# x and out laid out in DRAM as in SBUF, the first tiles loaded whole and split by halves, unused matmuls ahead of and between the first tiles

## Chip, core and metric

The kernel runs on one core of one Trainium2 chip. The metric is device time in microseconds (us), the median of several executions. Besides these there is one profiled execution, from which every row below comes.

## What is computed

The reference takes x (8 batches of 1024 nodes with 128 features, f32) and adj (1024 x 1024). It has two layers, each `x = layernorm(x + layer(x))`.

- Layer 0: with A2 = adj*adj (element by element), `h = relu(A2 @ (x @ W1))`, `h = relu(A2 @ (h @ W2))`, `A2 @ (h @ W3)`. W1 is 128 x 256, W2 is 256 x 512, W3 is 512 x 128.
- Layer 1: two graph convolutions `relu(adj @ (h @ Wg + bg))`, and then LSTMs over windows of 1, 2, 3 and 4 nodes, each of which overwrites the last node of its windows.

The change touches how layer 0 begins, and how x is read and the result is written.

## The kernel before

**Numbers in two parts.** Each f32 matrix is split into a rounded part HI and a rest LO. ScalarE (ACT) writes HI as a copy into the matmul format; VectorE (DVE) writes LO as source minus HI. A product is then three matmuls (HI*HI, HI*LO, LO*HI; `product`, lines 593 to 595). One of 512 columns is a matmul of `128x512`.

**Start of layer 0.** adj comes as eight row tiles of 128 x 1024 (512 KB each) into `square`, where it is squared in place, partly by ACT (tiles 1, 2, 4, 6 and the right half of tile 0, line 941), partly by DVE (left half of tile 0, tiles 3, 5, 7, line 1180). ACT then writes HI (line 945) and DVE writes LO (line 1112). The node features of batches 0 and 1 are split in the same way (line 948 for HI, 1112 for LO) into `node` and `node_b`, first those of two node tiles (`x0 first`, `x1 first`), the other six later (`x0 rest`, `x1 rest`). The list `PRE` (line 205) names the order in which these parts become ready; ACT counts them in `a_hi`, DVE in `a_lo`, and both engines work through them strictly in that order. TensorE (PE) waits with `prepared_by_now(name)`.

**PE at the start.** After 18 unused transposes of the identity (line 754) it goes tile by tile (m = 0 to 7, lines 656 to 660): for each it adds, for both halves of columns, batch 0's product and then batch 1's, 12 matmuls of 512 columns in all, into four PSUM banks. All later work of layer 0 (pairs of batches, four pairs) and layer 1 follows in one order that is written out by hand.

**The DMA queue.** All loads and stores are issued by SyncE (SP) on one queue, in this order at the start: left half of adj tile 0, x0 first, right half of tile 0, x1 first, tile 1, x0 rest, tile 2, tile 3, x1 rest, tile 4, w1, tiles 5 to 7, w2, w3, the other six batches of x, small weights. In DRAM x is (batch, node, feature), so that one SBUF partition takes runs of 128 floats, 512 bytes each; an adj row is 4 KB in one run. The result goes out in the same node-major layout, one store for each batch but the last, which is stored in two parts (line 561) when DVE has scaled four node tiles each (line 1172). The program ends when the last has landed.

Of the kernel before, what the change touches and what calls it, by code (L numbers as in the profile page):

```python
# [39 lines left out]
def build(nc, x, adj_t, w1, w2, w3, wg0, bg0, wg1, bg1, wih_t, whh_t, bih, bhh, out):  # L40
    B, N, F = x.shape
    H1, H2 = w1.shape[1], w2.shape[1]
# [8 lines left out]
    with ctx:  # L51
# [100 lines left out]
        def sem(name):  # L152
            return ctx.enter_context(nc.semaphore(name))

        x_first_in = [sem("x0_first_in"), sem("x1_first_in")]
        x_rest_in = [sem("x0_rest_in"), sem("x1_rest_in")]
        adj0_left_in = sem("adj0_left_in")
        xr_in = sem("xr_in")
# [48 lines left out]
        X_FIRST = 2  # L207
        ACT_SQUARES = (1, 2, 4, 6)

        A_PRE = len(PRE) - 1  # L210

        def prepared(name):

            return PRE.index(name) + 1

# [303 lines left out]
        def _(sp):  # L519
            def load_x(j, tiles, landed):  # L520
                sp.dma_start(xb[:, j, tiles], x[j].rearrange("(t p) c -> p t c", p=P)[:, tiles]).then_inc(landed, 16)

            for half, landed in ((0, adj0_left_in), (1, adj_in[0])):
                cols = slice(half * BANK, (half + 1) * BANK)
                sp.dma_start(square[:, 0, cols], adj_t[0:P, cols]).then_inc(landed, 16)
                load_x(half, slice(0, X_FIRST), x_first_in[half])
            for m in range(1, MT):
# [9 lines left out]
            for b in range(2, B):  # L537
                sp.dma_start(xb[:, b], x[b].rearrange("(t p) c -> p t c", p=P)).then_inc(xr_in, 16)
            for k, small in enumerate((wg0, wg1, bg0, bg1)):
# [9 lines left out]
            def store(b, done):  # L549

                sp.wait_ge(out_ready, b + 2)
                sp.dma_start(out[bass.ds(b, 1)].rearrange("b (t p) c -> p (b t) c", p=P),
                             xb[:, bass.ds(b, 1)].rearrange("p b t c -> p (b t) c")).then_inc(done, 16)
# [36 lines left out]
        def _(pe):  # L590
# [16 lines left out]
            def pair_products(it, first=False):  # L607
# [28 lines left out]
                for j in range(2):  # L636
# [4 lines left out]
                    if first:  # L641

                        def prepared_by_now(name):
                            lo_reached(prepared(name) - A_PRE)

                        def both_halves(of, q0, m):
                            for half in range(HALVES):
                                if m == 0:
                                    prepared_by_now(("adj0 left", "adj0 right")[half])
                                last = product(ps[:, (q0 + half) % BANKS, :], lambda i: of[:, i, m * P:(m + 1) * P],  # L650
                                               lambda i: adj[:, i, m, half * BANK:(half + 1) * BANK],
                                               m == 0, m == MT - 1)
                                if m == MT - 1:
                                    last.then_inc(a_mm, 1)

                        for m in range(MT) if j == 0 else ():
                            prepared_by_now("x0 first" if m == 0 else f"adj{m}")
                            both_halves(node, 0, m)
                            prepared_by_now("x1 first" if m < X_FIRST else "x1 rest")
                            both_halves(node_b, A_MM, m)  # L660
# [69 lines left out]
                for m in range(MT):  # L730
# [199 lines left out]
        def _(act):  # L930
# [6 lines left out]

            def adj_hi(m, cols, squared):
                if squared is None:

                    nc.scalar.activation(square[:, m, cols], square[:, m, cols], ACT.Square).then_inc(sq_act, 1)
                    act.wait_ge(sq_act, m // 2 + 2 if m > 1 else m + 1)
                else:
                    act.wait_ge(sq_done, squared)
# [6 lines left out]
            adj_hi(0, slice(0, BANK), 1)  # L951
            act.wait_ge(x_first_in[0], 16)
            x_part_hi(node[:, HI, 0:X_FIRST * P], xb[:, 0, first])
            act.wait_ge(adj_in[0], 16)
            adj_hi(0, slice(BANK, N), None)
            act.wait_ge(x_first_in[1], 16)
            x_part_hi(node_b[:, HI, 0:X_FIRST * P], xb[:, 1, first])
            for m in range(1, MT):
                if m in ACT_SQUARES:
                    act.wait_ge(adj_in[m], 16)  # L960
                adj_hi(m, slice(0, N), None if m in ACT_SQUARES else (m + 1) // 2)
                if m in (1, 2):
                    act.wait_ge(x_rest_in[m - 1], 16)
                    x_part_hi((node, node_b)[m - 1][:, HI, X_FIRST * P:], xb[:, m - 1, rest])
                if m == 4:
                    act.wait_ge(w1_in, 16)
                    nc.scalar.activation(w1s[:, HI, :], w0_raw[:, 0:H1], ACT.Copy).then_inc(a_hi, 1)
            act.wait_ge(w0_in, 32)
# [139 lines left out]
        def _(dve):  # L1108
# [79 lines left out]

            left, right = slice(0, BANK), slice(BANK, N)
            tail = slice(X_FIRST * P, N)  # L1190
            nc.vector.memset(took_wait[:, 0:1], 0.0).then_inc(out_ready, 1)
            square_part(adj0_left_in, 0, left)
            dve.wait_ge(a_hi, prepared("adj0 left"))
# [6 lines left out]
            x_part_lo(node_b[:, LO, 0:X_FIRST * P], xb[:, 1, 0:X_FIRST], node_b[:, HI, 0:X_FIRST * P])  # L1200
            for m in range(1, MT):
                if m == 2:
                    square_part(adj_in[3], 3, slice(0, N))
                dve.wait_ge(a_hi, prepared(f"adj{m}"))
                adj_lo(m, slice(0, N))
                if m in (1, 2):
                    dve.wait_ge(a_hi, prepared(f"x{m - 1} rest"))
                    of = (node, node_b)[m - 1]
                    x_part_lo(of[:, LO, tail], xb[:, m - 1, X_FIRST:], of[:, HI, tail])
                if m in (3, 4):  # L1210
                    square_part(adj_in[2 * m - 1], 2 * m - 1, slice(0, N))
                if m == 4:
                    dve.wait_ge(a_hi, prepared("w1"))
                    lo_part(w1s[:, LO, :], w0_raw[:, 0:H1], w1s[:, HI, :], a_lo)
            dve.wait_ge(a_hi, prepared("w2 w3"))
# [318 lines left out]
```

## Time and profile before

| | |
|---|---|
| time, 3 executions | median 1026.88 us, 1026.53 to 1027.72 |
| the profiled execution | 1026.49 us |
| its span (first to last instruction) | 1024.7 us |
| PE busy | 993.9 us, 97% |
| DVE busy | 571.5 us, 56% |
| ACT busy | 374.7 us, 37% |
| mean granted TensorE clock | 0.99 of full speed |

The device time is 1.8 us more than the span: what lies around the program's instructions. Busy shares are means over the whole; in the first 15 us and in the last 60 us PE waits, in the stretch between it hardly does.

### The profile page before, as it was taken

To read this page: it belongs to the slowest core of one execution; us is meant where nothing else is said; L and a number is where in the kernel's file an instruction comes from. 1 tells how busy PE (TensorE), PEld (TensorE's weight loads), DVE (VectorE), ACT (ScalarE), POOL (GpSimd) and SP (SyncE) were. 2 spreads that over 40 slices of the span, in tenths; PEclk is the share of its full clock that TensorE was granted. 3 is DMA by queue.
4 is the path that set the end of the run, shared out by engine and by line. 5 is a ranking of instruction groups with operands and counts; after the bars stand their busy time and mean duration, and the time that the engine had idled before them with its cause. 6 is when DMAs were issued, how large, how long until landed. Compare 5 with 4: busy or idle time off the path is not lost.

```text
span 1024.7 us, 14363 instructions
## 1 busy us (share of the span) xinstructions
PE 993.9 (97%) x5386; PEld 867.1 (85%) x5386; DVE 571.5 (56%) x1357; ACT 374.7 (37%) x680; POOL 19.8 (2%) x22
## 2 busy tenths in 40 slices
PE   8999999999999999999999999999999999999882
PEld 6888998889988899888897889898989889889882
DVE  7242353323443234332486556877686777877887
ACT  7231111221112220222334444555464544646551
POOL 0000000000000000000000000101010100100000
PEclk9999999999999999999999999999999999999897
DMA  9400000000000000000220000000000000000001
GB/s 313 135 1 0 1 1 1 1 1 1 1 0 0 0 0 0 0 0 0 82 82 1 1 1 2 0 2 21 1 1 21 0 21 0 21 5 17 1 21 42
DMA packets 21919, 20.42 MB, mean 20 GB/s; under 512 B 1008, under 2 KB 18544, under 8 KB 21872
## 3 DMA queue, kind: packets, MB, share of 16 engines
q1 hardware_dynamic: 21872, 19.81, 6.1%
q8 instruction: 27, 0.44, 0.2%
q14 instruction: 20, 0.16, 0.1%
HBM read 15.61 MB, written 4.19 MB: 19 GB/s over the span
## 4 chain that ended last, share of the span: by engine, by line
PE 91%; DVE 6%; ACT 1%; DMA 1%; issue 0%; SPq 0%; DVEq 0%; ACTq 0%
PE ps L593 27%; PE ps L594 27%; PE ps L595 27%; PE ps L742 9%; DMA square<-in_adj_t 1%; PE ps L633 1%; PE ps L921 1%; ACT gates_last L1052 0%; DVE gates_last L1396 0%; PE ps L762 0%; DVE xb L1172 0%; DVE stats L1129 0%; ACT gates_last L1062 0%; DVE xb L1474 0%; DVE gates L1396 0%
## 5 line engine op out<-in xcount | busy, mean ns | idle before, releaser
L593 PE MATMUL ps<-adj,node 128*128 128x512 f32 x368 | 144.7, 393 | 3.2 <-DVE adj L1112 1.9
L594 PE MATMUL ps<-adj,node 128*128 128x512 f32 x368 | 143.5, 390 | 0.0
L595 PE MATMUL ps<-adj,node 128*128 128x512 f32 x368 | 143.5, 390 | 0.0
L1112 DVE TENSOR_TENSOR y<-ps,y 128x512 fp32r<-128x512 f32 x46 | 31.8, 692 | 174.1 <-ACT y L984 174.1
L984 ACT ACTIVATE y<-ps 128x512 fp32r<-128x512 f32 x46 | 27.5, 598 | 271.8 <-PE ps L595 271.7
L593 PE MATMUL ps<-adj,h 128*128 128x512 f32 x256 | 99.7, 389 | 0.0
L594 PE MATMUL ps<-adj,h 128*128 128x512 f32 x256 | 99.7, 389 | 0.0
L595 PE MATMUL ps<-adj,h 128*128 128x512 f32 x256 | 99.6, 389 | 0.0
L1115 DVE SCALAR_TENSOR_TENSOR h<-ps,h 128x512 fp32r<-128x512 f32 x112 | 76.4, 689 | 40.2 <-ACT h L984 39.4
L742 PE MATMUL ps<-s,adj 128*128 128x256 f32 x768 | 93.7, 283 | 0.0
L742 PEld LDWEIGHTS ps<-s,adj 128*128 128x128 f32 x768 | 92.9, 192 | 0.3
L1052 ACT ACTIVATE gates<-ps,lb 128x512 f32<-128x512 f32 (+2 forms) x117 | 70.8, 648 | 42.2 <-PE ps L595 32.3
L593 PEld LDWEIGHTS ps<-adj,node 128*128 128x128 f32 x368 | 69.1, 188 | 18.8 <-DVE adj L1112 3.2
L984 ACT ACTIVATE h<-ps 128x512 fp32r<-128x512 f32 x96 | 57.4, 598 | 69.7 <-PE ps L595 66.9
L595 PEld LDWEIGHTS ps<-adj,node 128*128 128x128 f32 x368 | 69.1, 188 | 14.8
L594 PEld LDWEIGHTS ps<-adj,node 128*128 128x128 f32 x368 | 69.2, 188 | 13.1
L1052 ACT ACTIVATE gates_x<-ps,lb 128x258 f32<-128x258 f32 (+1 forms) x156 | 67.1, 508 | 34.3 <-PE ps L595 34.2
L595 PEld LDWEIGHTS ps<-adj,h 128*128 128x128 f32 x256 | 48.1, 188 | 10.0
L593 PEld LDWEIGHTS ps<-adj,h 128*128 128x128 f32 x256 | 48.1, 188 | 9.8
L594 PEld LDWEIGHTS ps<-adj,h 128*128 128x128 f32 x256 | 48.1, 188 | 9.7
L595 PE MATMUL ps<-y,w2s 128*128 128x512 f32 x128 | 49.8, 389 | 0.0
L593 PE MATMUL ps<-y,w2s 128*128 128x512 f32 x128 | 49.8, 389 | 0.0
(233 smaller groups left out, 1981.7 us busy)
## 6 DMA issues: line engine op xcount, KB each, us to landing
adj_raw<-in_adj_t SPq DMA_DIRECT2D x8, 512.0 KB, 6.9
square<-in_adj_t SPq DMA_DIRECT2D x7, 512.0 KB, 8.5
out<-xb SPq DMA_DIRECT2D x7, 512.0 KB, 3.2
xb<-in_x SPq DMA_DIRECT2D x6, 512.0 KB, 8.0
lw_raw<-in_wih_t SPq DMA_DIRECT2D x1, 1024.0 KB, 5.6
xb<-in_x SPq DMA_DIRECT2D x2, 384.0 KB, 7.2
lw_raw<-in_whh_t SPq DMA_DIRECT2D x1, 768.0 KB, 7.1
square<-in_adj_t SPq DMA_DIRECT2D x2, 256.0 KB, 3.2
```

The lines of the kernel that those rows point to most:

```text
L593: pe.matmul(dst, stat(HI), mov(HI), start=start, stop=False)
L594: pe.matmul(dst, stat(HI), mov(LO), start=False, stop=False)
L595: return pe.matmul(dst, stat(LO), mov(HI), start=False, stop=stop)
L633: last = pe.transpose(ps[:, q % BANKS, t * F:(t + 1) * F], s3t[:, nt:nt + P], ident_f[:])
L742: last = pe.matmul(dst, adj[:, a, m, nt:nt + P], s3[:, b, m, :, :].rearrange("p j c -> p (j c)"), start=(m == 0 and t == 0 and (a, b) == ( ...
L921: last = pe.transpose(ps[:, GB + n_fin % 2, (t - t0) * F:(t - t0 + 1) * F], full_in(slot, back)[:, at:at + P], ident_f[:])
L984: nc.scalar.activation(dst, ps[:, (j * A_MM + q) % BANKS, :], func).then_inc(a_hi, 1)
L1052: nc.scalar.activation(gates_in(u.stream)[:, g, at], ps[:, (AHEAD["gate"][slot] + gate) % GB, 0:u.n], ACT.Tanh if g == GG else ACT.Sigmoid ...
L1112: nc.vector.tensor_tensor(dst, src, f32(hi), ALU.subtract).then_inc(done, 1)
L1115: nc.vector.scalar_tensor_tensor(out=dst, in0=src, scalar=0.0, in1=f32(hi), op0=ALU.max, op1=ALU.subtract).then_inc(done, 1)
```

## The change

- **Layout.** The host hands x over as (batch, 128 partitions, node tile, feature), which is how it lies in SBUF, and the result comes back in that shape. For one batch a partition reads or writes one run of 4 KB (2 KB for each part of the last batch) where it had 8 (4) runs of 512 bytes. The loads of `square` and of the weights keep theirs.
- **Loads.** adj tile 0, all of x0, all of x1 and adj tiles 1 to 7 are one DMA each (w1 is still behind tile 4).
- **Order of the split.** x0 rest now stands ahead of adj tile 1, x1 rest behind tile 2. Tile 1 is split by halves too. In tiles 0 and 1 ACT squares one half and DVE the other.
- **PE.** 13 unused products of 512 columns replace the 18 transposes; they wait for a memset of their operand by DVE. 2 more follow tile 0, and 2 more stand ahead of tile 2. Tile 1 goes half by half (both batches for the left half, then both for the right).

```diff
-        PRE = ["adj0 left", "x0 first", "adj0 right", "x1 first", "adj1", "x0 rest", "adj2", "x1 rest", "adj3", "adj4",
-               "w1", "adj5", "adj6", "adj7", "w2 w3"]
+        PRE = ["adj0 left", "x0 first", "adj0 right", "x1 first", "x0 rest", "adj1 left", "adj1 right", "adj2",
+               "x1 rest", "adj3", "adj4", "w1", "adj5", "adj6", "adj7", "w2 w3"]
...
+            def load_x(j):
+                sp.dma_start(xb[:, j], x[j]).then_inc(x_in[j], 16)
+
+            for m in range(MT):
                 sp.dma_start(square[:, m, :], adj_t[m * P:(m + 1) * P, :]).then_inc(adj_in[m], 16)
-                if m in (1, 3):
-                    load_x(m // 2, slice(X_FIRST, MT), x_rest_in[m // 2])
+                if m == 0:
+                    load_x(0)
+                    load_x(1)
...
-                sp.dma_start(out[B - 1].rearrange("(t p) c -> p t c", p=P)[:, t0:t1, :],
+                sp.dma_start(out[B - 1][:, t0:t1, :],
                              xb[:, B - 1, t0:t1, :]).then_inc(out_done, 16)
...
+                        for m in range(MT) if j == 0 else ():
+                            if m == 0:
+                                prepared_by_now("adj0 left")
+                                prepared_by_now("x0 first")
+                                by_half(node, 0, m, 0)
+                                prepared_by_now("adj0 right")
+                                by_half(node, 0, m, 1)
+                                idle_products(IDLE[0])
+                                prepared_by_now("x1 first")
+                                by_half(node_b, A_MM, m, 0)
+                                by_half(node_b, A_MM, m, 1)
+                                idle_products(IDLE[1])
+                                continue
+                            if m < HALVED:
+                                for half in range(HALVES):
+                                    prepared_by_now(f"adj{m} {('left', 'right')[half]}")
+                                    by_half(node, 0, m, half)
+                                    by_half(node_b, A_MM, m, half)
+                                continue
+                            if m == HALVED:
+                                idle_products(IDLE[2])
...
+            IDLE = (0, 2, 2)
+
+            def idle_products(n):
+                for _ in range(n):
+                    pe.matmul(ps[:, BANKS - 3, :], s3[:, HI, 0, 0, :],
+                              s3[:, HI, 0:2].rearrange("p t j c -> p (t j c)"), start=True, stop=True)
+
+            pe.wait_ge(warm_set, 1)
+            idle_products(13)
             pe.wait_ge(eye_set, 2)
-
-            for _ in range(18):
-                pe.transpose(ps[:, BANKS - 3, 0:P], ident_f[:], ident_f[:])
...
+            square_here(0, right)
+            act.wait_ge(sq_done, 1)
+            adj_hi(0, left)
+            act.wait_ge(x_in[0], 16)
             x_part_hi(node[:, HI, 0:X_FIRST * P], xb[:, 0, first])
+            adj_hi(0, right)
+            act.wait_ge(x_in[1], 16)
             x_part_hi(node_b[:, HI, 0:X_FIRST * P], xb[:, 1, first])
+            x_part_hi(node[:, HI, X_FIRST * P:], xb[:, 0, rest])
+            square_here(1, left)
+            adj_hi(1, left)
+            act.wait_ge(sq_done, 2)
+            adj_hi(1, right)
+            square_here(2, whole)
+            adj_hi(2, whole)
...
+            square_part(adj_in[1], 1, right)
+            dve.wait_ge(a_hi, prepared("x0 rest"))
+            x_part_lo(node[:, LO, tail], xb[:, 0, X_FIRST:], node[:, HI, tail])
+            dve.wait_ge(a_hi, prepared("adj1 left"))
+            adj_lo(1, left)
+            dve.wait_ge(a_hi, prepared("adj1 right"))
+            adj_lo(1, right)
+            square_part(adj_in[3], 3, whole)
+            dve.wait_ge(a_hi, prepared("adj2"))
+            adj_lo(2, whole)
```

## Rows read from the trace of the kernel before

**Rows 1.** The page: the chain of work that ended last, shares by engine
```profile
PE 91%; DVE 6%; ACT 1%; DMA 1%; issue 0%; SPq 0%; DVEq 0%; ACTq 0%
```

**Rows 2.** PE's waits over the whole span: total us, times, longest us
```profile
PE ps L593 <- DVE hw_last L1112: 3.1, 1, 3.1
...
PE ps L593 <- DVE adj L1112: 1.9, 3, 1.1
...
PE ps L593 <- DVE node L1112: 1.2, 2, 0.8
```

**Rows 3.** The chain that ended last, 0 to 16 us: start us, us, what
```profile
4.29 7.57 DMA square<-in_adj_t
...
11.88 1.23 DVE square L1180
13.11 1.15 DVE adj L1112
...
14.30 0.50 PE ps L593
```

**Rows 4.** PE's timeline at the start: start us, us, engine, line, operation
```profile
6.01 0.50 PE L593 MATMUL ps<-adj,node 128*128 128x512 f32 x1 [0.82 <-DVE node L1112]
...
11.02 0.49 PE L593 MATMUL ps<-adj,node 128*128 128x512 f32 x1 [1.06 <-DVE adj L1112]
...
13.66 0.39 PE L595 MATMUL ps<-adj,node_b 128*128 128x512 f32 x1
```

**Rows 5.** The timeline of SP's DMA issues, same columns
```profile
0.81 0.39 SPq L525 DMA_DIRECT2D square<-in_adj_t  x1
...
4.80 0.74 SPq L521 DMA_DIRECT2D xb<-in_x  x1
```

**Rows 6.** DMA issues of 0.8 to 1.2 and 4.8 to 5.5 us: count, KB, us to landing
```profile
square<-in_adj_t SPq DMA_DIRECT2D x1, 256.0 KB, 2.7
...
xb<-in_x SPq DMA_DIRECT2D x1, 384.0 KB, 8.4
```

**Rows 7.** Stretches: us, busy PE PEld DVE ACT POOL, clock, DMA share, GB/s
```profile
2.00:8.00 6.00, 4.54 (x22) 3.78 (x21) 2.75 (x5) 3.04 (x7) 0.00 (x0) 1.00 0.98 301
8.00:12.00 4.00, 2.94 (x13) 2.11 (x12) 2.21 (x3) 3.86 (x5) 0.00 (x0) 1.00 1.05 376
...
14.00:16.00 2.00, 1.76 (x8) 1.42 (x8) 2.00 (x3) 1.97 (x4) 0.00 (x0) 1.00 1.01 402
26.00:28.00 2.00, 2.00 (x10) 1.65 (x9) 0.00 (x0) 0.00 (x0) 0.00 (x0) 1.00 1.19 293
```

**Rows 8.** Timelines of ACT and DVE in the preparation, by shape
```profile
4.93 0.69 DVE L1112 TENSOR_TENSOR adj<-square,adj 128x512 fp32r<-128x512 f32 x1 [0.70 <-ACT adj L945]
5.54 0.63 ACT L941 ACTIVATE square<-square 128x512 f32<-128x512 f32 x1 [0.33 <-DMA square<-in_adj_t]
...
10.52 1.06 ACT L941 ACTIVATE square<-square 128x1024 f32<-128x1024 f32 x1
...
10.88 0.95 DVE L1112 TENSOR_TENSOR node<-xb,node 128x768 fp32r<-128x768 f32 x1
```

**Rows 9.** The unused transposes, 1.4 to 5.2 us: ns min/median/max
```profile
L754 PE MATMUL ps<-ident_f x18: 272/418/473, 1.4 to 4.9; 128*128 128x128 f32 x18
```

**Rows 10.** PE's timeline around 969 us, two neighbours
```profile
969.24 0.49 PE L593 MATMUL ps<-hw_last,lw 128*128 128x344 f32 x1
969.52 0.49 PE L594 MATMUL ps<-hw_last,lw 128*128 128x344 f32 x1
```

**Rows 11.** A stretch around that place, columns as in rows 7
```profile
969.00:970.00 1.00, 1.00 (x5) 1.00 (x4) 0.88 (x2) 0.46 (x1) 0.00 (x0) 0.50 0.00 0
```

**Rows 12.** The end: timeline of the last two stores
```profile
1020.03 1.42 SPq L561 DMA_DIRECT2D out<-xb  x2
```

**Rows 13.** Their transfer, columns as in rows 7
```profile
1021.00:1023.00 2.00, 0.00 (x0) 0.00 (x0) 0.03 (x1) 0.00 (x0) 0.00 (x0) 0.50 0.90 259
```

**Rows 14.** Landing of the last store, columns as in rows 6
```profile
out<-xb SPq DMA_DIRECT2D x1, 256.0 KB, 3.1
```

More of the change, by code:

```diff
@@ L153, in sem @@
             return ctx.enter_context(nc.semaphore(name))
-        x_first_in = [sem("x0_first_in"), sem("x1_first_in")]
-        x_rest_in = [sem("x0_rest_in"), sem("x1_rest_in")]
-        adj0_left_in = sem("adj0_left_in")
+        x_in = [sem("x0_in"), sem("x1_in")]
+        warm_set = sem("warm_set")
         xr_in = sem("xr_in")
@@ L644, in prepared_by_now @@
                             lo_reached(prepared(name) - A_PRE)
-                        def both_halves(of, q0, m):
-                            for half in range(HALVES):
[L648 to L660, printed above, removed]
+                        def by_half(of, q0, m, half):
+                            last = product(ps[:, (q0 + half) % BANKS, :], lambda i: of[:, i, m * P:(m + 1) * P],
+                                           lambda i: adj[:, i, m, half * BANK:(half + 1) * BANK],
+                                           m == 0, m == MT - 1)
+                            if m == MT - 1:
+                                last.then_inc(a_mm, 1)
@@ new lines, in pair_products @@
+                        for m in range(MT) if j == 0 else ():
[19 more added lines that the diff above has]
+                                idle_products(IDLE[2])
+                            prepared_by_now("x0 rest")
+                            prepared_by_now(f"adj{m}")
+                            for half in range(HALVES):
+                                by_half(node, 0, m, half)
+                            prepared_by_now("x1 rest")
+                            for half in range(HALVES):
+                                by_half(node_b, A_MM, m, half)
@@ L935, in x_hi, with square_here, adj_hi @@
                                      ACT.Copy).then_inc(done, 1)
[L938 to L944, printed above, removed]
+            squares = [0]
+            def square_here(m, cols):
+                act.wait_ge(adj_in[m], 16)
+                nc.scalar.activation(square[:, m, cols], square[:, m, cols], ACT.Square).then_inc(sq_act, 1)
+                squares[0] += 1
+                act.wait_ge(sq_act, squares[0])
+            def adj_hi(m, cols):
                 nc.scalar.activation(adj[:, HI, m, cols], square[:, m, cols], ACT.Copy).then_inc(a_hi, 1)
@@ L950, in _ @@
             first, rest = slice(0, X_FIRST), slice(X_FIRST, MT)
-            adj_hi(0, slice(0, BANK), 1)
-            act.wait_ge(x_first_in[0], 16)
+            left, right, whole = slice(0, BANK), slice(BANK, N), slice(0, N)
+            square_here(0, right)
+            act.wait_ge(sq_done, 1)
+            adj_hi(0, left)
+            act.wait_ge(x_in[0], 16)
             x_part_hi(node[:, HI, 0:X_FIRST * P], xb[:, 0, first])
-            act.wait_ge(adj_in[0], 16)
-            adj_hi(0, slice(BANK, N), None)
-            act.wait_ge(x_first_in[1], 16)
+            adj_hi(0, right)
+            act.wait_ge(x_in[1], 16)
             x_part_hi(node_b[:, HI, 0:X_FIRST * P], xb[:, 1, first])
[L958 to L967, printed above, removed]
+            x_part_hi(node[:, HI, X_FIRST * P:], xb[:, 0, rest])
[5 more added lines that the diff above has]
+            adj_hi(2, whole)
+            x_part_hi(node_b[:, HI, X_FIRST * P:], xb[:, 1, rest])
+            act.wait_ge(sq_done, 3)
+            adj_hi(3, whole)
+            square_here(4, whole)
+            adj_hi(4, whole)
+            act.wait_ge(w1_in, 16)
+            nc.scalar.activation(w1s[:, HI, :], w0_raw[:, 0:H1], ACT.Copy).then_inc(a_hi, 1)
+            act.wait_ge(sq_done, 4)
+            adj_hi(5, whole)
+            square_here(6, whole)
+            adj_hi(6, whole)
+            act.wait_ge(sq_done, 5)
+            adj_hi(7, whole)
             act.wait_ge(w0_in, 32)
@@ L1187, in x_part_lo @@
                 lo_part(dst, src.rearrange("p t c -> p (t c)"), hi, a_lo)
-            left, right = slice(0, BANK), slice(BANK, N)
+            left, right, whole = slice(0, BANK), slice(BANK, N), slice(0, N)
             tail = slice(X_FIRST * P, N)
+            nc.vector.memset(f32(s3[:, HI, 0:2]), 1.0).then_inc(warm_set, 1)
             nc.vector.memset(took_wait[:, 0:1], 0.0).then_inc(out_ready, 1)
-            square_part(adj0_left_in, 0, left)
+            square_part(adj_in[0], 0, left)
             dve.wait_ge(a_hi, prepared("adj0 left"))
@@ L1200, in _ @@
             x_part_lo(node_b[:, LO, 0:X_FIRST * P], xb[:, 1, 0:X_FIRST], node_b[:, HI, 0:X_FIRST * P])
-            for m in range(1, MT):
-                if m == 2:
-                    square_part(adj_in[3], 3, slice(0, N))
-                dve.wait_ge(a_hi, prepared(f"adj{m}"))
[L1205 to L1214, printed above, removed]
+            square_part(adj_in[1], 1, right)
[8 more added lines that the diff above has]
+            adj_lo(2, whole)
+            dve.wait_ge(a_hi, prepared("x1 rest"))
+            x_part_lo(node_b[:, LO, tail], xb[:, 1, X_FIRST:], node_b[:, HI, tail])
+            dve.wait_ge(a_hi, prepared("adj3"))
+            adj_lo(3, whole)
+            square_part(adj_in[5], 5, whole)
+            dve.wait_ge(a_hi, prepared("adj4"))
+            adj_lo(4, whole)
+            dve.wait_ge(a_hi, prepared("w1"))
+            lo_part(w1s[:, LO, :], w0_raw[:, 0:H1], w1s[:, HI, :], a_lo)
+            square_part(adj_in[7], 7, whole)
+            for m in range(5, MT):
+                dve.wait_ge(a_hi, prepared(f"adj{m}"))
+                adj_lo(m, whole)
             dve.wait_ge(a_hi, prepared("w2 w3"))
```

25 lines of the change are left out of this document (9 added, 16 removed).

## The prediction

> **What bounds the kernel now.** The first view to read is the chain that ended last: PE holds 91% of it [rows 1], so only what delays PE, or what follows its last matmul, can move the time. The second is the list of PE's waits over the whole span [rows 2]. Its three waits for `adj` (1.9 us together, 1.1 at most) all lie in the first 15 us; the other large ones, such as 3.1 us for `hw_last`, belong to the LSTM steps near 968 us, which the change leaves alone. The third is the chain in order of time [rows 3]: the load of adj tile 3 lands at 4.29 + 7.57 = 11.86, DVE squares that tile (1.23 us), only then does it write LO of tile 2, and PE begins tile 2 at 14.30. From there on PE has work without a gap, as no later wait for `adj` is in the list. So the whole head of the kernel is worth one number: the time T at which PE begins tile 2 with nothing late behind it, 14.30 now. The timeline [rows 4] shows what stands ahead: first real product at 6.01, tile 1 from 11.02 until its last matmul at 13.66 plus 0.23, that is 2.87 us for the 12.
>
> **The loads.** By the issues [rows 5, 6] the left half of tile 0 lands at 0.81 + 2.7 = 3.5 and x1 rest at 4.80 + 8.4 = 13.2. The latter comes 1.3 us behind tile 3, its neighbour in the queue; 384 KB in 1.34 us are 293 GB/s, and the stretch in which only x is loaded shows 293 too, against 402 where it is mostly adj rows [rows 7]. So 512-byte runs move at 293, 4 KB runs at 402.
> Ahead of tile 3's landing there are now 2,688 KB (640 of x), and with the change 3,072 KB (1,024 of x).
> - Slow end: the rest keeps its pace and only x changes its rate. Before, 655e3 bytes at 293 = 2.24 us; after, 1,049e3 at 402 = 2.61. Tile 3 lands 0.4 later, 12.2.
> - Fast end: everything moves at 402 from the start. Bytes begin to move at about 2.0. Up to 11.86 the stretches of rows 7 give 6.0 x 301 + 3.86 x 376 = 3.26 MB moved, of which 2.75 MB are landed: a lag of 0.5 MB, 1.3 us. After: 2.0 + 3.146 MB / 402 (7.8 us) + 1.3 = 11.1.
> I take 11.6, near the middle: the 301 GB/s of the first 6 us are only partly x, so part of that slowness stays. In the same way (bytes ahead, and a lag growing from 0.2 MB at the first landing to 0.5) whole tile 0 lands at 4.2 (3.9 to 4.6), x0 at 5.7, x1 at 7.3, tile 1 at 8.9 (8.3 to 9.5), tile 2 at 10.3.
>
> One rule of the Trainium skill speaks against this: DMA: Bandwidth & Descriptors, Specifications, puts the smallest transfer for line rate at 512 bytes, so longer runs would bring nothing. Rows 7 differ (293 against 402). By that rule the 384 KB more would come on top, and its price is that of the rival "x no faster" below.
>
> **The preparation, walked through.** Durations [rows 8]: 128x512 0.63 on ACT and 0.69 on DVE, 128x1024 1.06 and 1.23 [rows 3], x rest about 0.85 and 0.95; consecutive ones start about 0.1 before the former ends.
> - Tile 0: ACT squares the right half and DVE the left (4.2 to 4.9), HI left to 5.5, LO left to 6.2, x0 first (landed 5.7) HI to 6.1, LO to 6.6. First real product at 6.6 against 6.01. It is late by 0.6, which is not on the path: the right half follows at 7.4, batch 1 (x1 landed 7.3, LO at 8.2) ends at 9.7, and tile 1 is not there.
> - x0 rest, now ahead of tile 1: HI 7.7 to 8.5 on ACT beside the wait for tile 1, so at no cost.
> - Tile 1 from 8.9: ACT squares left to 9.6, HI left to 10.2, HI right to 10.8; DVE squares right to 9.6, writes LO of x0 rest (0.9) to 10.5, LO left to 11.1, LO right to 11.7. PE begins tile 1 at 11.15 (now 11.02); halves buy PE a start 0.6 earlier than the whole tile would give, and the later landing and x0 rest take it back.
> - Tile 2: DVE squares tile 3 11.65 to 12.85, ACT has HI of tile 2 at 12.85, LO is ready at 14.1. PE: 11.15 + 2.8 for 12 matmuls = 13.95, then 2 unused products of 0.23 = 14.4. **T = 14.4 (now 14.30): +0.1.** The unused pair ahead of tile 2 is on the path, since it holds PE 0.3 past the data.
> - Later tiles: LO of tile 3 at 16.1 against PE's need at 14.4 + 2.75 = 17.2; LO of tile 5 at about 21 against 22.6. x1 rest (LO 14.95) is needed at 15.8. The cover is 0.8 us or more; if it were gone, each us of lateness would be one us of time.
> With landings at the fast end T = 13.8 (-0.5), at the slow end with tile 1 at 9.5 it is 15.0 (+0.7).
>
> **Unused products.** Their memset replaces the wait for the identity: they start at about 1.4 as now. The 18 transposes took 418 ns at first and 272 at the end [rows 9]: TensorE ran at its lower clock (1.2 GHz) for some 3 us of them and then at 2.4. At the lower clock 344 columns take 0.28 to the next [rows 10], with a granted clock of 0.50 [rows 11], so 512 take 0.42; 13 are 5.5 us if the clock never rises and about 4.4 if it rises near 4.7, as now. They end between 5.8 and 6.9; real work is ready at 6.6. Cost 0 to 0.3 for the first product, hidden by PE's wait for tile 1.
>
> The Trainium skill (TensorE: Matmul & The Clock Gate, Part 4) says that transposes don't count as busy for the clock; by it only the change would wake the clock early. The row shows the clock rise while nothing but transposes had run. Its result is the rival "clock late before" below.
>
> **The stores.** The last two parts are issued from 1020.03, 1.42 us for both [rows 12]; they move at 259 GB/s for 2 us [rows 13], and the last lands 3.1 after its issue [rows 14]. No row shows stores in longer runs. Bound: no gain (259 stays), or 402 for the last 262e3 bytes, 0.65 instead of 1.0 us; the first part is then done before the second is ready to move, so no more than that is saved: 0 to -0.4. I take -0.3, as loads show that run length sets the rate. The other stores and the loads of batches 2 to 7 are shorter too, but wait for nobody.
>
> **Sum.** Against the profiled execution: +0.1 - 0.3 = -0.2, span 1024.5, with the 1.8 around it 1026.3. The profiled execution is 0.4 under the median of the runs; the same offset gives **1026.7 us**.
>
> **Rivals.**
> - *x no faster.* 393e3 bytes more at 293 = 1.3 us: tile 3 lands at 13.2, T = 15.6; stores unchanged. 1028.2, slower, though still within 0.2%. It decides once a 512 KB load of x takes 1.8 us instead of 1.3; it would also be so if the new layout were still cut into 512-byte runs. For it: no row shows x in long runs. Against: 4 KB adj rows at 402. Chance 9%.
> - *The clock falls at the start.* Should the early wait of PE or the late first product leave it at the lower clock until past 12 us, tile 0 (9 matmuls of 0.42 from 6.9) ends at 10.7, with 2 unused 11.5, tile 1 takes 5.1, and two more unused give T = 17.4: +3.1 - 0.3, so 1029.7. It decides where the lower clock lasts beyond about 11. For it: the clock did fall near 967 us, around a wait of 3.1 us [rows 2, 11]. Against: PE is busy nearly without a break from 1.4 to 8. Chance 5%.
> - *Clock late before.* If in most executions of the kernel before the clock rose only after tile 1, tile 1 would end at 11.02 + 12 x 0.42 = 16.1, 1.8 later than profiled, and the change would give that back: 1024.7. Against: the profiled execution is one of four within 1.2 us. Chance 6%.
> - *Fast loads.* T = 13.8, stores -0.4: 1026.0. Within my forecast's own range.
>
> **Chances.** Forecast (T within -0.5 and +0.7, stores 0 to -0.4) 80%, x no faster 9%, clock falls 5%, clock late before 6%. 0.2% is 2.05 us, about what can be told from no change; only the clock cases reach it: faster 6%, within 88%, slower 6%. Range for 8 in 10: the forecast's sum from 1026.0 to 1027.4 and 0.6 for the spread of the runs, 1025.4 to 1028.1.
>
> **What would show it.** Landing of tile 3 near 11.6 and of x0, x1 1.3 to 1.6 us apart: right. PE's tile 2 beginning at 14.4 right behind two unused products, not behind a DVE wait: right. First real product at 6.6. Last store landing some 2.8 after its issue. Wrong: tile 2 waiting for DVE beyond 15, a wait of PE for tiles 3 to 7, matmuls of 512 columns 0.42 apart after 8 us, or a difference anywhere between 20 and 1010 us other than where the clock falls once.

## The result: 1025.1 us, faster by about 0.2%, and the profile after

| | before | after |
|---|---|---|
| median (8 runs each, one after the other on one chip) | 1026.70 us | 1025.08 us |
| lowest, highest | 1026.40, 1027.72 | 1023.06, 1026.02 |
| the profiled execution, its span | 1026.49, 1024.7 | 1024.83, 1023.1 |
| from the issue of the last two stores to the end of the span | 4.6 | 3.5 |

The ratio is 0.9979, 95% interval 0.9970 to 0.9988: 2.2 us less (1.2 to 3.1). The forecast was 1026.7 with a range from 1025.4, so the time fell out of the range at the low end. The most probable outcome in the forecast, no measurable difference, was the wrong one.

First the shares of the chain in the changed kernel's page, beside [rows 1]: nothing moved there that the eye could catch.
```profile
PE 92%; DVE 5%; ACT 1%; DMA 1%; issue 0%; SPq 0%; DVEq 0%; ACTq 0%
```
Then its chain in order of time, as [rows 3] (start us, us, what):
```profile
2.19 7.35 DMA square<-in_adj_t
...
9.57 0.69 DVE square L1218
10.26 0.87 DVE node L1150
11.13 0.61 DVE adj L1150
11.74 0.04 issue
11.78 0.50 PE ps L589
...
14.58 0.23 PE ps L591
14.80 0.45 PE ps L773 x2
15.26 0.23 PE ps L589
```
The chain now runs through tile 1 (issued at 2.19, landed at 9.54), and tile 2 begins behind the two unused products, as forecast, and not behind a wait for DVE. But the timeline of PE puts that start at 15.09, later than the 14.30 of [rows 4] and than the 14.4 forecast:
```profile
1.53 4.59 PE L773 MATMUL ps<-s 128*128 128x512 f32 x13 [1.53 <-DVE s L1229]
6.78 0.47 PE L589 MATMUL ps<-adj,node 128*128 128x512 f32 x1 [0.67 <-DVE node L1150]
...
9.03 0.50 PE L589 MATMUL ps<-adj,node_b 128*128 128x512 f32 x1 [0.63 <-DVE node_b L1150]
...
11.78 0.50 PE L589 MATMUL ps<-adj,node 128*128 128x512 f32 x1 [0.61 <-DVE adj L1150]
...
14.64 0.62 PE L773 MATMUL ps<-s 128*128 128x512 f32 x2
15.09 0.39 PE L589 MATMUL ps<-adj,node 128*128 128x512 f32 x1
```
So one profiled execution is faster by 1.7 us than another although it starts 0.8 later. The end explains part of it. SP's issue and what landed (KB, us from issue to landing), as [rows 12, 14]:
```profile
1019.57 1.38 SPq L557 DMA_DIRECT2D out<-xb  x2
...
out<-xb SPq DMA_DIRECT2D x2, 256.0 KB, 2.1
```
Both parts now take 2.1, where the last took 3.1 [rows 14]. And of the wait for `hw_last` near 968 us [rows 10, 11] the stretch 969 to 976 tells the rest (columns: PE, PEld, DVE, ACT and POOL busy with counts, the granted clock, DMA share, GB/s), first of the kernel after, then of the kernel before:
```profile
969.00:976.00 7.00, 7.00 (x36) 6.98 (x37) 6.01 (x26) 2.91 (x7) 0.00 (x0) 0.76 0.00 0
```
```profile
969.00:976.00 7.00, 7.00 (x32) 6.94 (x31) 5.09 (x18) 2.54 (x6) 0.00 (x0) 0.64 0.00 0
```
The clock is at 0.5 for 3.4 us after and for 6.8 us before. That is worth 1.1 us in this pair of profiles, but it goes with the execution and not with the kernel: the kernel before has 3.4 us in both further profiles below, and a changed kernel (`a_noidle`) has 6.8. Three of the 17 profiles below (`b_prod`, `a_oldx`, `a_x1late`) have no fall there at all. From PE's start behind the wait for `hw_last` to its start behind the wait for `hstep_last` near 982 us it takes 12.1 us without a fall, 13.0 to 13.1 with 3.4 us and 14.1 to 14.2 with 6.8.

### The profile page after: what moved, and what is told of

It reads as the page before. It is cut to its first block, busy times and chain, and to the rows that moved or that the text cites. A ratio compares the mean times of both kernels' runs of the same rounds, so it can differ in the third digit from the quotient of the medians.

```text
span 1023.1 us, 14364 instructions
## 1 busy us (share of the span) xinstructions
PE 994.3 (97%) x5385; PEld 866.7 (85%) x5385; DVE 572.5 (56%) x1360; ACT 373.9 (37%) x681; POOL 19.8 (2%) x22
## 4 chain that ended last, share of the span: by engine, by line
PE 92%; DVE 5%; ACT 1%; DMA 1%; issue 0%; SPq 0%; DVEq 0%; ACTq 0%
PE ps L589 27%; PE ps L590 27%; PE ps L591 27%; PE ps L759 9%; DMA square<-in_adj_t 1%; PE ps L629 1%; PE ps L945 1%; ACT gates_last L1090 0%; PE ps L786 0%; ACT gates L1090 0%; DVE xb L1210 0%; DVE gates_last L1444 0%; DVE stats L1167 0%; DVE xb L1522 0%; DVE node L1150 0%
## 5 line engine op out<-in xcount | busy, mean ns | idle before, releaser
L590 PEld LDWEIGHTS ps<-adj,node 128*128 128x128 f32 x368 | 69.2, 188 | 13.2
## 6 DMA issues: line engine op xcount, KB each, us to landing
w_raw<-in_w SPq DMA_DIRECT2D x1, 512.0 KB, 11.7
```

What stands on the lines that cost most here:

```text
L590: pe.matmul(dst, stat(HI), mov(LO), start=False, stop=False)
```

## The experiments

All ran beside the kernel before on the same chip; its median was 1026.6 to 1027.2. Line numbers from here on are those of each kernel. Kernels named `b_` start from the kernel before, `a_` from the changed one. One table for all; "tile 1" is the moment at which ACT begins to square it (0.02 to 0.03 behind the landing, where ACT waited for it), T the start of tile 2 on PE, "last store" issue to landing. "Span minus T" holds the fall near 968 us too, so before and a_noidle have 1.2 to 1.5 more there than their likes, and b_prod, a_oldx and a_x1late, without a fall, some 0.4 less (0.9, of which 0.4 or more comes back behind 982 us).

| profiled execution | tile 1 | T | T minus tile 1 | last store | span minus T |
|---|---|---|---|---|---|
| before (profile above) | 7.56 | 14.30 | 6.74 | 3.1 | 1010.4 |
| look_b1 | 9.29 | 15.88 | 6.59 | 3.1 | 1009.1 |
| look_b2 | 8.69 | 15.63 | 6.94 | 3.2 | 1009.2 |
| b_out | 9.06 | 15.66 | 6.60 | 3.2 | 1009.3 |
| b_dve3 | 8.71 | 15.36 | 6.65 | 2.3 | 1008.3 |
| b_dve3b | 7.25 | 14.16 | 6.91 | 2.3 | 1008.4 |
| b_both | 8.65 | 16.43 | 7.78 | 3.2 | 1009.2 |
| b_prod | 8.88 | 16.79 | 7.91 | 2.3 | 1007.7 |
| after | 9.57 | 15.09 | 5.52 | 2.1 | 1008.0 |
| look_a | 8.15 | 13.69 | 5.54 | 2.1 | 1008.0 |
| a_oldout | 9.07 | 14.59 | 5.52 | 2.4 | 1008.4 |
| a_sp3 | 8.79 | 14.35 | 5.56 | 2.1 | 1008.5 |
| a_noidle | 9.67 | 14.85 | 5.18 | 2.1 | 1009.5 |
| a_transp | 9.34 | 14.51 | 5.17 | 2.1 | 1008.1 |
| a_oldx | 9.90 | 15.07 | 5.17 | 2.1 | 1007.7 |
| a_x1late | 8.46 | 13.63 | 5.17 | 2.0 | 1007.6 |
| a_whole | 9.36 | 17.28 | 7.92 | 2.1 | 1008.0 |

**look_b1, look_b2, look_a: the same kernels once more.** No edit.

> The kernel before, unchanged, one more look. Theory E (the execution profiled before the prediction was early at the head: its tile 1 landed at 7.5, where the four kernels with the same order of loads show 8.6 to 9.1): tile 1 lands at 8.5 to 9.1, tile 2 begins at 15.2 or later, last landing 3.1. Rival (those four are late by their edits): 7.5 and 14.3 again.

> The kernel before once more, with the same expectations: tile 1 lands at 8.5 to 9.1 and tile 2 begins at 15.2 or later by theory E, 7.5 and 14.3 by its rival.

> The changed kernel unchanged, one more look. If its profiled execution was a usual one, tile 1 lands at 9.3 to 9.7 us, PE begins tile 2 at 14.5 to 15.1, and the last store lands 2.1 us after its issue. If the spread of the loads is as wide as in the kernel before (7.5 to 9.3), tile 1 may land anywhere from 8 to 10.

Measured 1027.00, 1026.74 and 1023.49 us. The chain of look_b1 over its first 17 us:
```profile
2.71 6.55 DMA square<-in_adj_t
...
9.29 1.06 ACT square L941
10.38 1.06 ACT adj L945
11.46 1.23 DVE adj L1112
12.69 0.87 DVE node L1112
13.56 1.14 DVE square L1180
14.70 1.14 DVE adj L1112
```
Tile 1 lands at 9.27 here instead of 7.54. From there ACT and DVE have six pieces of work one right behind the other, 6.6 us together, and PE gets tile 2 when the last is done. In [rows 3] the chain is another: tile 1 was so early that DVE was done with the pieces ahead of squaring tile 3 just before this landed at 11.86, and so tile 3 set T, 2.44 behind its landing. look_b2 shows the same with tile 3 landing at 13.19, though its tile 1 came at 8.67:
```profile
4.29 8.90 DMA square<-in_adj_t
...
14.44 1.15 DVE adj L1112
```
So two chains of nearly the same length lead to T in the kernel before: tile 3's in three profiles (before, look_b2, b_dve3b) and tile 1's in three (look_b1, b_out, b_dve3). The same loads, issued at nearly the same times, land up to 2 us apart from one execution to the next (tile 1 at 7.2 to 9.3, tile 3 at 11.7 to 13.2), and T comes 6.6 to 6.9 behind tile 1 by either chain. The six profiled executions with the old order of loads and of splits and x's old layout have T at 14.16 to 15.88, mean 15.17. The profile on which the prediction was built was one of the two early ones. The four with the new order and both unused pairs have 13.69 to 15.09, mean 14.43. The chain of look_a shows the other face of the same thing:
```profile
9.89 0.45 PE ps L773 x2
...
10.37 0.50 PE ps L589
...
13.40 0.45 PE ps L773 x2
13.86 0.23 PE ps L589
```
From 6.92 on PE is released by no other engine that was late: its own order and the unused pairs fill the chain. Tile 1, landed at 8.13, was ready at just that moment: its first product comes 2.22 behind the start of its squaring, as in the others. Both pairs take 0.45 each; what the second costs is read below, from kernels without it.

**b_out, a_oldout: the layout of the result alone, one way and the other.**
```diff
-                sp.dma_start(out[B - 1].rearrange("(t p) c -> p t c", p=P)[:, t0:t1, :],
+                sp.dma_start(out[B - 1][:, t0:t1, :],
```


> The kernel before, with the new layout for out alone. Theory S (the stores are the gain: in the profile of the changed kernel they end 1.1 us sooner after their issue, and the head is later by 0.6 to 0.8): 1025.6, the last store landing about 2.1 after its issue. Rival C (the gain is in the clock: one stretch at the lower clock near 970 us is 3.4 us long in the changed kernel and 6.8 in the one before, and the unused products bring that about): stores give 0.3, 1026.4. Rival L (loads at the head): no gain, 1026.7.

> The changed kernel with out in the old layout. Theory S: it loses 1.1, 1026.2, within 0.6 of the kernel before and perhaps slower than it by the head's 0.6 where the clock falls alike. Rival C: it keeps most of the gain, 1025.4. Rival L: 1025.4 too.

b_out 1027.01 us, ratio 0.9999 (0.9990 to 1.0008); a_oldout 1025.09 us, 0.9979 (0.9970 to 0.9988), which is what the changed kernel itself has. The layout of the result is worth nothing that can be measured in the time. It takes 0.3 to 0.4 off a store of 256 KB: the first of the two takes 2.4 in the short runs (before) and 2.0 in the long ones (b_out). But it doesn't explain the last store: b_out has the long runs and still takes 3.2, a_oldout has the short ones and takes 2.4. Something else held the last store. The DMA view of the last microseconds of the kernel before (a row of GB/s in 40 slices of 50 ns, then the queues):
```profile
GB/s 123 205 287 297 338 307 266 287 266 297 440 276 256 297 297 276 256 216 164 72 10 20 20 20 0 10 10 10 10 0 10 10 20 31 10 0 0 0 0 0
...
q1 hardware_dynamic: 533, 0.26, 46.8%
q14 instruction: 1, 0.01, 1.6%
```
In the slice with 440 the transfer of another queue falls into the store: q14, which brings instructions, 8 KB. Nearly all of the store is done half a microsecond later, but a trickle of 10 to 30 GB/s goes on for another 0.8 us. b_out shows both as well.

**b_dve3, b_dve3b: three more instructions on DVE.** q14 has 20 such transfers in the page after; when one comes depends on how far an engine is in its instructions. Built, the kernel before has 1373 instructions on DVE and the changed one 1376. So the kernel before got three more that do nothing:
```diff
+            dve.wait_ge(adj_in[1], 16)
+            dve.wait_ge(adj_in[2], 16)
...
+            dve.wait_ge(adj_in[6], 16)
```


> The kernel before with six waits on DVE at 25 us that are long satisfied (three instructions more, as the changed kernel has). In the kernel before and its two variants so far the last store lands 3.1 to 3.2 us after its issue, the first of the pair 2.0 to 2.4; in the changed kernel and its variants both land 2.1 to 2.4 after it, whatever the layout of out. Theory F (an 8 KB load of instructions, there in the trace during the last store of the first three kernels and 2 us ahead of it in the others, holds up one of the store's 16 parts, and it is the place in DVE's instruction stream that sets when it comes): last landing 2.4, time 1.0 less than the kernel before, 1025.8. Rival P (the place in SP's stream, or chance, sets it): landing 3.1, time as before, 1026.8.

> The kernel before with three more instructions on DVE (waits for adj tiles that have long landed), a repeat of b_dve3. Theory: they move DVE's last instruction load out of the last store, whose landing is 2.3 us instead of 3.2, so the median is about 0.9 us less, 1025.9 beside 1026.8. Rival: the landing is shorter but the time is the same, 1026.8, because the last store has its delay only in some executions or the rest of the program differs by more.

Now the 8 KB come at 1017.7, some 2 us ahead of the two issues, and nothing trails (b_dve3; the first line is of 1017 to 1018, the others of 1020 to 1024, in slices of 100 ns):
```profile
q14 instruction: 1, 0.01, 3.2%
...
GB/s 0 0 0 0 0 0 0 0 36 236 323 276 302 282 302 276 271 200 103 154 297 307 276 307 266 317 276 277 149 10 0 0 0 0 0 0 0 0 0 0
...
out<-xb SPq DMA_DIRECT2D x2, 256.0 KB, 2.4
```
The last landing is 2.3 in both, and span minus T falls from 1009.2 (look_b1, look_b2, b_out) to 1008.35. In the times: b_dve3 1026.65 us, 0.9994 (0.9985 to 1.0003); b_dve3b 1026.14 us, 0.9996 (0.9987 to 1.0005). Either alone is "no difference". The 22 runs of both together have a mean 0.59 us below that of the 46 runs of before beside them (resampled interval 0.22 to 0.99); by medians it is 0.48, with an interval that holds zero. The theory's 0.9 is near the upper end of that. The rest of the forecast (2.3 or 2.4 instead of 3.2) held.

**a_sp3: the same on SP, in the changed kernel.** Three instructions more on SP bring it to the 77 of the kernel before.
```diff
+            sp.wait_ge(adj_in[0], 16)
...
+            sp.wait_ge(adj_in[5], 16)
```


> The changed kernel with six satisfied waits on SP ahead of the stores (three instructions more, as many as the kernel before has). Theory F with DVE's stream: nothing changes, landing 2.1, 1025.1. Rival P (SP's stream): the last store lands 3.1 after its issue, 1026.1.

1024.50 us, 0.9970 (0.9959 to 0.9981), last store 2.1. It is DVE's stream that matters, not SP's. The other profiles agree: the five with 1373 instructions on DVE (before, look_b1, look_b2, b_out, b_both) have q14's transfer inside the last store, which takes 3.1 to 3.2; the twelve with more have it ahead, and the store takes 2.0 to 2.4. One more is enough, as b_prod and a_whole show with 1374.

**b_both: both layouts in the kernel before, its order kept.**
```diff
-                sp.dma_start(xb[:, j, tiles], x[j].rearrange("(t p) c -> p t c", p=P)[:, tiles]).then_inc(landed, 16)
+                sp.dma_start(xb[:, j, tiles], x[j][:, tiles]).then_inc(landed, 16)
```


> The kernel before with the new layout for x and out; order of loads, of the split and of PE as before (x first in 1 KB runs, x rest in 3 KB runs). Theory S: as b_out, and the head earlier: 640 KB of x at 402 instead of 293 GB/s bring tile 3 0.6 sooner, so 1025.0 and PE's tile 2 at 13.7 instead of 14.30; this would beat the changed kernel. Rival C: 1026.0, tile 2 earlier. Rival L (whole loads and the new order are what helps): not under 1026.0.

1026.21 us, 0.9993 (0.9984 to 1.0002), runs from 1024.5 to 1028.6. Tile 1 comes at 8.65, no earlier than usual, but tile 0 is done sooner, so PE waits 2.62 us in one piece, and the granted clock falls:
```profile
11.00:12.00 1.00, 0.00 (x0) 0.00 (x0) 1.00 (x2) 1.00 (x2) 0.00 (x0) 0.93 1.05 426
12.00:15.00 3.00, 2.89 (x7) 2.31 (x8) 3.00 (x4) 2.97 (x4) 0.00 (x0) 0.50 1.03 411
```
T is 7.8 behind tile 1, 1.0 more than in the others. Here is the prediction's rival of a falling clock, at a third of its price.

Whether the layout of x helps the kernel before stays open. b_both lies 0.8 us below b_out, run on the same chip, by the means, with a resampled interval of -0.1 to 1.7, and its eleven runs spread over 4 us.

**a_oldx: only x's layout taken back** (in a changed kernel without the unused pairs).
```diff
-                sp.dma_start(xb[:, j], x[j]).then_inc(x_in[j], 16)
+                sp.dma_start(xb[:, j], x[j].rearrange("(t p) c -> p t c", p=P)).then_inc(x_in[j], 16)
```


> The changed kernel without the unused products between the tiles, and with x in DRAM node by node (512-byte runs) as before, still loaded whole per batch. Theory: x moves at 293 instead of about 400 GB/s, tile 1 lands about 1.0 us later (10.3 instead of 9.3), PE begins tile 2 at about 15.8 and the time is about 1025.4. Rival: x's layout makes no difference, tile 1 lands at 9.3 to 9.6 and the time is 1024.4 as with the new layout.

1024.56 us, 0.9980 (0.9970 to 0.9989), where a_noidle, the same with the new layout, has 1024.39, 0.9976 (0.9967 to 0.9985). Tile 1 at 9.90 against 9.67: its landing 7.5 us after its issue, in the changed kernel 7.4.
```profile
2.35 7.53 DMA square<-in_adj_t
...
9.90 0.69 DVE square L1218
```
The rival expectation held, but it is no proof of nothing: beside the kernel before on its own chip a_oldx is 0.4 us slower than a_noidle by the means, with an interval of -0.2 to 1.1, and one profile each says little where landings spread by 1.5. What the layout does to the loads the two profiles do show (columns as in rows 7), first old, then new layout:
```profile
2.00:8.00 6.00, 5.36 (x17) 3.88 (x17) 2.49 (x4) 2.29 (x5) 0.00 (x0) 1.00 0.99 314
18.00:30.00 12.00, 12.00 (x55) 9.93 (x54) 7.91 (x9) 5.76 (x7) 0.00 (x0) 1.00 1.19 291
```
```profile
2.00:8.00 6.00, 5.92 (x19) 4.30 (x18) 2.40 (x4) 2.30 (x5) 0.00 (x0) 1.00 0.97 340
18.00:30.00 12.00, 12.00 (x55) 9.94 (x54) 7.68 (x8) 6.00 (x7) 0.00 (x0) 1.00 1.05 387
```
From 18 to 30 us, when mostly batches 2 to 7 of x are loaded, the queue moves 291 GB/s with x in runs of 512 bytes and 387 with x in runs of 4 KB (301 and 385 in b_out and b_both), but nothing waits for them. In the first 8 us, where PE waits for loads, it is 314 and 340: the head is slow in either layout, and 26 GB/s over 6 us are 0.16 MB, some 0.4 us, an estimate from these rows.

**a_noidle, a_transp: without the unused pairs, and with the old transposes at the start.**
```diff
-            IDLE = (0, 2, 2)
+            IDLE = (0, 0, 0)
```


> The changed kernel without the two unused products after tile 0 and the two ahead of tile 2 (the 13 at the start stay). Theory S: the pair ahead of tile 2 is on the path, so PE's tile 2 begins 0.45 sooner (14.6), time 0.4 less than the changed kernel, 1024.7. Rival C (unused products hold the clock up): the clock would fall at the head or be later to rise, time 1025.1 or more, with matmuls 0.42 apart after 8 us.

> The changed kernel with the 18 transposes of before in place of the 13 unused products, and none between the tiles. Theory H: in part of the executions the clock rises late or falls while PE waits for tile 1, so the median is 0.5 to 1 above the kernel without unused products between the tiles (1024.4): 1025.1, with a wide spread. Rival (products bring nothing): 1024.4, as that kernel.

a_noidle 1024.39 us, 0.9976 (0.9967 to 0.9985). a_transp, with 18 transposes in place of the 13 products too, 1024.26 us, 0.9967 (0.9955 to 0.9980). T comes 5.2 behind tile 1 without the pairs and 5.5 with them. The pair ahead of tile 2 costs 0.35, and the unused products bring nothing that can be told in the time.

**b_prod: 13 unused products instead of the transposes, in the kernel before.**
```diff
+            for _ in range(13):
+                pe.matmul(ps[:, BANKS - 3, :], s3[:, HI, 0, 0, :],
+                          s3[:, HI, 0:2].rearrange("p t j c -> p (t j c)"), start=True, stop=True)
-            for _ in range(18):
-                pe.transpose(ps[:, BANKS - 3, 0:P], ident_f[:], ident_f[:])
```


> The kernel before with 13 unused products of 512 columns in place of the 18 transposes (and the memset for them). Theory H (before, the clock rises at 5 us in some executions and at 10 to 15 in others, so that tile 2 begins between 14.3 and 16.4; the denser start keeps it up): tile 2 at 14.3 to 15.2, all matmuls of 512 columns after 8 us at 0.23; time 0.7 less than before, 1026.1, and 1.0 less on top only if the last store lands sooner. Rival (the order of loads and split is what fixes the head): 1026.8.

1026.12 us, 0.9992 (0.9982 to 1.0001), runs from 1024.9 to 1029.8. The products do one thing reliably: in all nine profiled executions that open with them the first real products take 0.4 to 0.5. Of the eight that open with transposes, four (look_b2, b_out, b_dve3, a_transp) show what look_b2 does:
```profile
1.43 4.10 PE L754 MATMUL ps<-ident_f 128*128 128x128 f32 x18 [1.43 <-POOL ident_f L571]
6.14 0.80 PE L593 MATMUL ps<-adj,node 128*128 128x512 f32 x1 [0.61 <-DVE node L1112]
6.74 0.63 PE L594 MATMUL ps<-adj,node 128*128 128x512 f32 x1
```
A product every 0.42 instead of 0.23 is the lower clock (1.2 GHz), and it stays until 10 or 11 us. Yet T is not later for it: look_b2's 6.94 and b_out's 6.60 behind tile 1 are the usual distance, since tile 0's products have the room. In look_b1 the clock had risen at 4.8 and fell again from 8.2 to 11.6, in the middle of tile 0; this too cost nothing at T. In b_prod itself PE waits 2.32 us for tile 1, the clock fell at 13.4, in the middle of tile 1, and T is 7.9 behind it.

**a_whole: tile 1 squared and split whole again** (no pairs between).
```diff
-            square_here(1, left)
-            adj_hi(1, left)
-            act.wait_ge(sq_done, 2)
-            adj_hi(1, right)
+            square_here(1, whole)
+            adj_hi(1, whole)
```


> The changed kernel without unused products between the tiles, and with tile 1 split whole. Theory E: from the landing of tile 1 to PE's tile 2 there are 1.09 (square) + 1.06 (HI) on ACT and 1.15 + 1.14 + 1.25 on DVE = 5.7 against 5.2 with halves and 6.7 in the kernel before, so 1.0 of the head's gain comes from x0 rest standing ahead of tile 1 and 0.5 from the halves: time 0.5 more than a_noidle (1024.4), 1024.9. Rival (halves bring nothing): 1024.4.

1026.20 us, 0.9984 (0.9975 to 0.9993), in two groups: five runs at 1024.1 to 1025.0 and six at 1026.2 to 1027.0. The profiled one belongs to the upper. From its timeline of PE and its stretches:
```profile
12.82 0.65 PE L589 MATMUL ps<-adj,node 128*128 128x512 f32 x1 [2.17 <-DVE adj L1142]
13.27 0.63 PE L590 MATMUL ps<-adj,node 128*128 128x512 f32 x1
```
```profile
11.00:13.00 2.00, 0.18 (x1) 0.18 (x2) 1.46 (x2) 1.97 (x3) 0.00 (x0) 1.00 1.03 400
13.00:16.00 3.00, 3.00 (x8) 2.32 (x9) 3.00 (x4) 3.00 (x4) 0.00 (x0) 0.50 1.02 414
```
PE begins tile 1 3.46 behind the start of its squaring (2.2 in the changed kernel), waits 2.17 us for it, and then runs it at the lower clock: T is 7.9 behind instead of 5.2. By the means the whole tile costs 1.3 us (1025.81 against 1024.51 of a_noidle, which ran on another chip; 1.1, with a resampled interval of 0.2 to 1.9, when each is taken against the kernel before beside it).

**a_x1late: six tiles of x1 moved behind tile 3**, no pairs between. In the changed kernel all of x1 is ahead of tile 1, though two of its eight tiles are needed there.
```diff
-                    load_x(0)
-                    load_x(1)
+                    load_x(0, slice(0, MT), x_in[0])
+                    load_x(1, slice(0, X_FIRST), x_in[1])
+                if m == 3:
+                    load_x(1, slice(X_FIRST, MT), x1_rest_in)
```


> The changed kernel without unused products between the tiles, x1 loaded as two tiles ahead of tile 1 and the rest behind tile 3. Theory E: 384 KB less ahead of tile 1 and tile 2, at 402 GB/s 1.0 us: tile 1 lands at 8.4 instead of 9.3, tile 3 as before less x1 rest, 1.0 earlier too; tile 2 begins at 13.9 to 14.1 instead of 14.8: 1023.6. Rival (DVE's and ACT's own work is the limit by now): 1024.4, with no wait of DVE for a landing after tile 1.

1023.46 us, 0.9966 (0.9954 to 0.9979), the lowest median of all, 3.5 us under the kernel before by the ratio.
```profile
2.19 6.24 DMA square<-in_adj_t
...
8.46 0.69 DVE square L1222
9.15 0.87 DVE node L1154
10.02 0.61 DVE adj L1154
...
10.68 0.50 PE ps L592
```
Tile 1 lands 6.2 after its issue instead of 7.4, and T is 13.63. It beats both kernels, though its interval overlaps that of the changed one. In this profile the clock doesn't fall near 968 us, which shortens its span by some 0.4 beyond what T explains; the median doesn't rest on that one execution.

## Why the prediction was wrong, by its own steps

- **"T = 14.4 (now 14.30): +0.1."** The walk of the changed kernel was right: tile 1 was put at 8.9 and T at 14.4; the four executions average 8.9 and 14.43, 5.5 apart as in the walk. What failed is "now 14.30". It was read from one execution as if it belonged to the kernel, but it belonged to lucky landings (tile 1 at 7.54, tile 3 at 11.86; the means of the six are 8.4 and 12.6), and the mean T is 15.17. The change is 1.2 quicker from tile 1 to T (6.7 to 5.5), and its tile 1 comes 0.5 later (8.43 to 8.90), with 768 KB more of x ahead of it: 0.7 sooner net, not 0.1 later. With six and four profiles that spread by 0.7 and 0.6 (standard deviation), the 0.7 is uncertain by about 1 either way.
- **"The profiled execution is 0.4 under the median of the runs; the same offset gives 1026.7 us."** The offset was taken as if it were the same for both kernels. It held two errors of opposite sign that nearly cancelled: T 0.9 early, and a clock low near 968 us for 3.4 us longer than usual (1.1 us late).
- **"halves buy PE a start 0.6 earlier than the whole tile would give".** Too small: 3.46 from the squaring of tile 1 to its first product in a_whole, 2.21 in the changed kernel, so 1.25.
- **The loads.** Rates by layout (293 against 402) were argued from stretches with different contents, and hold where the layout alone differs (291 against 387). So the rule that the prediction sets against them, by which runs longer than 512 bytes bring nothing, isn't borne out by these rows. But the rates don't govern the head, which moves 314 and 340 in its first 8 us. Of the landings in the changed kernel's profile, tile 0 is at 4.1 (4.2 forecast), x1 at 8.1 (7.3), tile 1 at 9.54 (8.9, bound 9.5), tile 3 at 12.1 (11.6); look_a has 6.9, 8.1 and 10.7 for the last three. The four average 11.4 for tile 3, so the forecast was good; but the kernel before averages 12.6, and tile 3 comes 1.2 sooner with 384 KB more ahead of it, where the sum had 0.3. Layout alone (b_both, 12.1) gives a part of that; the rest is not explained. x0 and x1 land 1.4 to 2.7 apart, not 1.3 to 1.6.
- **"I take -0.3, as loads show that run length sets the rate."** The layout takes 0.3 off the landing (2.4 to 2.1), as said, and nothing visible in the medians. The larger term, 0.8 us of an instruction load inside the last store, had no place in the sum. [Rows 13, 14] show its result, 3.1 for the last part; the other part took 2.4, and that difference was not followed.
- **The unused pair ahead of tile 2 "holds PE 0.3 past the data".** Right: 0.35.
- **"right behind two unused products"**: right. **First real product at 6.6**: 6.7 to 7.2 in the four. It costs nothing in three; in look_a it stands in the chain, which reaches tile 1 at the moment that this is ready.
- **Rival "clock late before", 6%.** Its number, 1024.7, was near, its mechanism not. The clock did rise late in three of the seven executions that keep the old order and opening, but T was no further behind tile 1 in them. Where the clock does cost (b_both 1.0 and b_prod 1.2 on T, and the upper group of a_whole) it fell behind a wait of PE for tile 1 of 2.2 to 2.6 us. That wait is 0.9 or less in the kernels with halves, which is what these seem to bring beside their own share. A long wait isn't the only occasion: in look_b1 the clock fell behind waits of 0.9 and 0.6.
- **Rivals "x no faster" and "clock falls at the start".** Neither came. The first is wrong in its premise: x does move faster in long runs, 512 KB of batches 2 to 7 landing 1.3 us apart in a_noidle and 1.7 to 1.9 in b_out. The second counts 9 matmuls for tile 0, which has 12: by its own steps T would be 18.6 and not 17.4.
- **The range.** T +0.7 and stores 0 add up to 1027.6, not 1027.4; this doesn't touch the low end, where the time fell out.

The Trainium skill (TensorE: Matmul & The Clock Gate, Part 4) has transposes not counting as busy for the clock. The forecast set that aside on one execution's rows. Over 17 executions the rows speak for it in part: the clock rose late in 4 of 8 openings by transposes, in none of 9 by products. In the other four openings by transposes it rose at 4.7 to 5.6, before any product had run. For the time it doesn't matter here (a_transp 1024.26, a_noidle 1024.39).

**The sum by what the runs showed.** Head 0.7; the instruction load 0.6 in the runs (0.85 in the profiles); layout of the result 0 to 0.3. Together 1.3 to 1.9, beside 2.2 (1.2 to 3.1) measured; the head's 0.7 is the least certain of the terms. That the head's gain hangs on the halves is shown by a_whole, which loses 1.1 to 1.3 without them; what the earlier place of x0 rest and the whole loads bring was not tried by itself, and x's layout may hold some tenths of it. Why tile 3 lands sooner in the changed kernel, why the loads land up to 2 us apart from one execution to the next, and how often q14's transfer meets the last store in runs without a profile, stay open.

## What to carry to other kernels

A single profiled execution is a sample: before a start-up is priced from it, look at a second one, and price the distance from a landing to the first work behind it, which repeats to 0.2 us here, not the landing, which moves by 2. See which landing the chain runs through: two can be nearly level, and one profile shows only one of them. When the last transfer of a kernel takes longer than its twin, look for another queue's packet in it. A rate that is right where a queue runs full is no price for a stretch in which it doesn't: read the rate of the stretch that is waited for.

## What the runs showed of the hardware

- Three instructions more in DVE's stream, which do nothing, take 0.8 to 0.9 us off the last store of this kernel (3.1 or 3.2 to 2.3). An 8 KB instruction load then comes ahead of the store and not inside it; in all 17 profiles the store takes 3.1 to 3.2 with that load inside and 2.0 to 2.4 without.
- The same loads in the same order landed tile 1 between 7.2 and 9.3 us in six executions.
- 18 transposes left TensorE at its lower clock until 10 or 11 us in four of eight executions, 13 products of 512 columns in none of nine.
- Behind the same wait of 3.05 us near 968 us the clock fell for 6.8 us in two profiles, for 3.4 in twelve and not at all in three; 3.4 us of it cost 0.9, 6.8 cost 2.0 to 2.1.
- From 18 to 30 us the loads move at 291 to 301 GB/s with x in runs of 512 bytes and at 385 to 387 in runs of 4 KB (a_oldx and b_out, a_noidle and b_both). A store of 256 KB takes 2.4 in runs of 512 bytes and 2.0 to 2.1 in runs of 2 KB. Neither made a difference to the time that could be told from the spread.
